# A recurrent cell over 256 steps: GpSimd also sums quarter 3, a new order of work, and TensorE's loop head at slot 0

## The reference, cut to what matters

```
encoded   = tanh(xt @ We + st @ Ue + be)                     # 24 values
new_state = tanh(xt @ Wx[c] + st @ Ws[c] + bk[c])            # 8 candidates of 32
mem       = [[encoded, err]] + mem[:-1]                      # the last 20 entries
agent_in  = relu(relu(mem @ enc_w1 + b1) @ enc_w2 + b2)      # 500 -> 64 -> 16
h1, c1    = lstm(agent_in, h1, c1);  h2, c2 = lstm(h1, h2, c2)
gate      = softmax(h2 @ gate_w + gate_b)
theta     = clamp01(2.5 * mean(|err| of the last 10 entries))
gate      = gate * theta + previous gate * (1 - theta)
st        = sum over c of gate[c] * new_state[c]
pred      = clamp01(st[31]);  err = pred - yt
```

## Time and profile before

| | us |
|---|---|
| median of 3 runs | 5925.37 (5924.08 to 5929.31) |
| the profiled execution | 5930.65 |
| its span | 5928.8 |
| TensorE busy / VectorE / ScalarE / GpSimd | 5535.1 / 4689.8 / 3831.1 / 1639.7 |
| mean granted TensorE clock | 0.979 of full speed |

### The profile page before, as it was taken

How to read it: one execution, slowest core, us unless ns; L and a number is a source line. 1 busy time by engine, 2 the same in 40 slices (tenths; PEclk the granted TensorE clock), 3 DMA queues, 4 the chain that set the end, 5 groups by cost and what they waited for, 6 DMA issues and landing times.

```text
span 5928.8 us, 184458 instructions
## 1 busy us (share of the span) xinstructions
PE 5535.1 (93%) x67584; PEld 3438.4 (58%) x67584; DVE 4689.8 (79%) x12854; ACT 3831.1 (65%) x9217; POOL 1639.7 (28%) x3588
## 2 busy tenths in 40 slices
PE   4999999999999999999999999999999999999998
PEld 2555555555555555555555555555555555555555
DVE  5878887887887887788788788788878878878887
ACT  2666666666666666666666666666666666666665
POOL 1222222222222222222222222222222222222222
PEclk9999999999999999999999999999999999999999
DMA  2111111111111111111111111111111111111111
GB/s 45 30 26 30 27 30 27 30 28 28 27 29 27 30 30 27 30 27 30 27 30 27 30 27 30 27 30 27 30 27 30 27 30 27 30 27 30 27 30 37
DMA packets 313074, 172.28 MB, mean 29 GB/s; under 512 B 171368, under 2 KB 278132, under 8 KB 312452
## 3 DMA queue, kind: packets, MB, share of 16 engines
q1 hardware_dynamic: 308724, 162.02, 10.4%
q10 hardware_dynamic: 3728, 0.15, 0.0%
HBM read 73.73 MB, written 2.10 MB: 13 GB/s over the span
## 4 chain that ended last, share of the span: by engine, by line
PE 71%; ACT 13%; DVE 9%; issue 6%; ACTq 1%; DMA 0%; POOL 0%; POOLq 0%; DVEq 0%
PE chain L442 16%; PE a_ps L404 10%; PE a_ps L393 8%; PE cand_ps L373 7%; PE cand_ps L364 7%; PE chain L429 6%; ACT a_sb L568 6%; ACT gates L593 4%; PE chain L338 4%; PE a_ps L415 4%; PE chain L459 4%; DVE cell_in L769 4%; DVE added L755 3%; PE cand_ps L359 3%; ACT tanh_c L599 2%
## 5 line engine op out<-in xcount | busy, mean ns | idle before, releaser
L393 PE MATMUL a_ps<-hist,w_hist 125*64 125x512 f16 x12288 | 1745.0, 389 | 80.9 <-DMA w_hist<-enc_table 80.9
L846 DVE TENSOR_REDUCE state<-mixed 128x64 f32<-128x512 f32 x2048 | 1353.3, 682 | 36.4 <-issue 2.4
L586 ACT ACTIVATE cand<-cand_ps 128x512 f32<-128x512 f32 x2048 | 1154.2, 590 | 184.6 <-PE cand_ps L373 184.6
L442 PE MATMUL chain<-cell_in,cell_w 128*64 128x128 f32 x16384 | 1092.9, 276 | 0.7 <-ACT cell_in L576 0.5
L442 PEld LDWEIGHTS chain<-cell_in,cell_w 128*64 128x64 f32 x16384 | 887.9, 136 | 288.8 <-ACT cell_in L576 181.4
L593 ACT ACTIVATE gates<-chain 128x512 f32<-128x512 f32 x1024 | 611.4, 597 | 619.7 <-PE chain L442 619.7
L959 POOL TENSOR_TENSOR err_ring<-pred_now,ys 128x8 f32 x512 | 122.0, 238 | 3129.6 <-DVE pred_now L853 3129.6
L393 PEld LDWEIGHTS a_ps<-hist,w_hist 125*64 125x64 f16 x12288 | 671.4, 112 | 526.1 <-issue 117.1
L755 DVE SCALAR_TENSOR_TENSOR added<-gates 128x256 f32<-128x256 f32 x1024 | 435.5, 425 | 445.2 <-ACT gates L593 445.2
L599 ACT ACTIVATE tanh_c<-gates 128x128 f32<-128x128 f32 x1024 | 316.9, 310 | 689.7 <-DVE gates L761 689.7
L769 DVE SCALAR_TENSOR_TENSOR cell_in<-gates,tanh_c 64x128 f32<-64x128 f32 x2048 | 585.7, 286 | 164.5 <-ACT tanh_c L599 150.9
(11 more groups left out here) (82 smaller groups left out, 6708.4 us busy)
## 6 DMA issues: line engine op xcount, KB each, us to landing
x_sb<-in_x_l SPq DMA_DIRECT2D x260, 256.0 KB, 2.8
hist<-entry_parts SPq DMA_DIRECT2D x2048, 25.0 KB
w_hist<-enc_table SPq DMA_DIRECT2D x258, 128.0 KB, 2.3
y_rows<-in_y_l SPq DMA_DIRECT2D x260, 8.0 KB
ys<-in_y SPq DMA_DIRECT2D x1, 2048.0 KB
preds_out<-preds SPq DMA_DIRECT2D x1, 2048.0 KB, 7.6
cell_w<-in_lstm_whh ACTq DMA_DIRECT2D x16, 3.0 KB
cell_w<-in_lstm_whh ACTq DMA_DIRECT2D x16, 1.0 KB
```

The source lines that it names most:

```text
L393: nc.tensor.matmul(a_ps[g][ENC * half:ENC * half + ENC, :], w_hist[0:HROWS, w_slot(u), kk, wp, :], hist[0:HROWS, xp, k, at:at + 512], star ...
L442: last = nc.tensor.matmul(chain[g][rows, P * r:P * r + P], cell_w[c][:, hf, r, :], cell_in[c][:, g, hf, :], start=False, stop=True, skip_g ...
L586: ins = nc.scalar.activation(cand[:, g, q // 2, :, q % 2, :, :].rearrange("p h s c -> p h (s c)"), cand_ps[q][:, :].rearrange("p (h k) -> ...
L846: V.tensor_reduce(state[:, g, hf, 2 * pair:2 * pair + 2, :], mixed[:, pair, hf, :, :, :], AX, ALU.add)\
```

## The change

- GpSimd gets `sum_of_quarter`: it adds the 8 candidates of quarter 3, both halves at once, by three additions (8 to 4, 4 to 2, 2 to 1), each waiting for the one before. `mix_sum` for pair 1 keeps quarter 2 alone. A semaphore `q_last` counts the new sums; `state_transpose`, `prediction` and the next `mix(1)` wait for it.
- The four phases of TensorE, ScalarE, VectorE and GpSimd are written in a new order, and some calls move from one item role to another (a call for `cur` that becomes one for `old` is made a phase later in the program).
- `CAND_ORDER` becomes (0, 2, 1, 3).
- TensorE's loop is given `head_slot` 0: its first instruction is to be loaded at slot 0 of an instruction fetch block.

```diff
+TENSOR_HEAD = 0
-CAND_ORDER = (2, 1, 3, 0)
+CAND_ORDER = (0, 2, 1, 3)
...
+        fours = sb("fours", [P, HF, S, 4])
+        twos = sb("twos", [P, HF, S, 2])
...
-            with nc.Fori(0, LOOPS, engines=[eng.engine], hint_back_edge=True) as turn:
+            with nc.Fori(0, LOOPS, engines=[eng.engine], hint_back_edge=True, head_slot=head_slot) as turn:
...
             def state_transpose(item, hf):
                 g, n, u = item
                 pe.wait_ge(q_sum[hf], SUMS * n)
+                pe.wait_ge(q_last, n)
```

TensorE's phase as it becomes (the old one is in the kernel above):

```diff
+                if old:
+                    cell_gates(old, 1)
+                if cur:
+                    state_transpose(cur, 0)
+                    state_transpose(cur, 1)
                 if new:
                     history_waits(new, old, extra)
                     history(new, 0)
+                if old:
+                    logit_bias(old)
+                if cur:
+                    encoded_s(cur)
+                if new:
+                    history(new, 1)
+                if old:
+                    gate_logits(old)
+                if cur:
+                    encoder1_now(cur)
+                    candidates_s(cur)
                     encoder2(cur)
                     bias_of_cell(cur, 0)
                 if new:
+                    history(new, 2)
                 if cur:
                     cell_gates(cur, 0)
+                if new:
+                    history(new, 3)
+                    encoded_x(new, old, extra)
+                if cur:
                     bias_of_cell(cur, 1)
                 if new:
+                    candidates_x(new, cur, extra)
+            run_phases(pe, phase, turn_start, {pe.engine: TENSOR_HEAD})
```

ScalarE's, and what is new on VectorE and GpSimd:

```diff
+                if old:
+                    candidates(old, 2)
+                    candidates(old, 1)
+                    cell_tanhs(old, 0)
+                    candidates(old, 3)
+                    value_tanh(old, 0)
+                    cell_tanhs(old, 1)
+                if cur:
+                    state_take(cur)
+                if old:
+                    value_tanh(old, 1)
+                if cur:
+                    at_least_zero(cur)
+                    encoded(cur)
+                if old:
+                    next_hidden(old)
+                if cur:
+                    entry_high(cur)
+                if old:
+                    exponentials(old)
+                if cur:
+                    encoder1(cur)
+                    candidates(cur, 0)
                     agent_input(cur)
...
+                if old:
+                    mix_sum(old, 0, 0)
+                if cur:
+                    cell_terms(cur, 0)
+                    cell_value(cur, 0)
+                if old:
+                    mix_sum(old, 0, 1)
                 if cur:
                     new_hidden(cur, 0)
                 if old:
+                    mix_sum(old, 1, 0)
                     mix_sum(old, 1, 1)
...
                 if cur:
                     peaks(cur)
                     below_peak(cur)
+                if new:
+                    error_sum(new)
+                    thetas(new)
+                if cur:
                     totals(cur)
...
+            def sum_of_quarter(item):
+                g, n, u = item
+                pool.wait_ge(q_mul[1], n + GROUPS if MIX_ORDER[1] == 1 else n)
+                G.tensor_tensor(fours[:, :, :, :], mixed[:, 1, :, 1, :, 0:4], mixed[:, 1, :, 1, :, 4:8], ALU.add)\
+                    .then_inc(q_fours, 1)
+                pool.wait_ge(q_fours, n)
+                G.tensor_tensor(twos[:, :, :, :], fours[:, :, :, 0:2], fours[:, :, :, 2:4], ALU.add)\
+                    .then_inc(q_twos, 1)
+                pool.wait_ge(q_twos, n)
+                G.tensor_tensor(state[:, g, :, 3, :], twos[:, :, :, 0], twos[:, :, :, 1], ALU.add)\
+                    .then_inc(q_last, 1)
...
                 if old:
-                    mix_quarter(old)
                     new_error(old, extra)
                     keep_prediction(old, extra)
-                if cur:
-                    kept_share(cur)
-                    kept_gate(cur)
                 if new:
                     entry_low(new)
                 if cur:
                     gate_in_sbuf(cur)
+                    mix_quarter(cur)
+                if new:
+                    kept_share(new)
+                    kept_gate(new)
+                if cur:
+                    sum_of_quarter(cur)
```

More of the change, by code:

```diff
@@ L140, in recurrent_kernel @@
                                     "inps", "in", "candps"))
+        q_fours, q_twos, q_last = (sem(f"q_{n}") for n in ("fours", "twos", "last"))
         q_keptfrom, q_mulpool = (sem(f"q_{n}") for n in ("keptfrom", "mulpool"))
@@ L160, in w_slot, with run_phases @@
             return u % PER_TILE
-        def run_phases(eng, phase, turn_start=None):
+        def run_phases(eng, phase, turn_start=None, head_slot=None):
             items = [None] * DEPTH
@@ L472, in phase @@
                 new, cur, old = items
+                if old:
+                    cell_gates(old, 1)
                 if cur:
-                    encoded_s(cur)
+                    state_transpose(cur, 0)
+                    state_transpose(cur, 1)
+                if new:
+                    history_waits(new, old, extra)
+                    history(new, 0)
                 if old:
@@ L482, in phase @@
                     encoder1_now(cur)
-                if new:
-                    history_waits(new, old, extra)
-                    history(new, 0)
-                if cur:
+                    candidates_s(cur)
                     encoder2(cur)
@@ L489, in phase @@
                 if new:
-                    history(new, 1)
+                    history(new, 2)
                 if cur:
                     cell_gates(cur, 0)
-                    candidates_x(cur, old, extra)
-                    candidates_s(cur)
+                if new:
+                    history(new, 3)
+                    encoded_x(new, old, extra)
+                if cur:
                     bias_of_cell(cur, 1)
                 if new:
[L497 to L505, removed]
+                    candidates_x(new, cur, extra)
+            run_phases(pe, phase, turn_start, {pe.engine: TENSOR_HEAD})
         @block.scalar
@@ L621, in phase @@
                 if cur:
[L622 to L628, removed]
-                if cur:
[L630 to L642, removed]
+                    entry_high(cur)
+                if old:
+                    exponentials(old)
+                if cur:
+                    encoder1(cur)
                     candidates(cur, 0)
+                    agent_input(cur)
             run_phases(act, phase)
@@ L845, in mix_sum @@
                     dve.wait_ge(q_mulpool, n + GROUPS)
-                V.tensor_reduce(state[:, g, hf, 2 * pair:2 * pair + 2, :], mixed[:, pair, hf, :, :, :], AX, ALU.add)\
-                    .then_inc(q_sum[hf], 1)
+                    V.tensor_reduce(state[:, g, hf, 0:2, :], mixed[:, 0, hf, :, :, :], AX, ALU.add)\
+                        .then_inc(q_sum[hf], 1)
+                else:
+                    V.tensor_reduce(state[:, g, hf, 2, :], mixed[:, 1, hf, 0, :, :], AX, ALU.add)\
+                        .then_inc(q_sum[hf], 1)
             def prediction(item):
@@ L864, in phase @@
                 if old:
-                    mix_sum(old, 0, 1)
+                    mix_sum(old, 1, 0)
                     mix_sum(old, 1, 1)
                 if cur:
-                    error_sum(cur)
                     cell_terms(cur, 1)
@@ L877, in phase @@
                 if cur:
-                    thetas(cur)
                     peaks(cur)
                     below_peak(cur)
+                if new:
+                    error_sum(new)
+                    thetas(new)
+                if cur:
                     totals(cur)
@@ L887, in phase @@
                     mix(cur, 0)
-                    mix_sum(cur, 1, 0)
-                if new:
-                    cell_terms(new, 0)
-                    cell_value(new, 0)
-                if cur:
-                    mix_sum(cur, 0, 0)
             run_phases(dve, phase, turn_start)
```

6 lines of the change are left out of this document (3 added, 3 removed).

## The result

The changed kernel takes 5894.02 us at the median of its runs (5892.56 to 5894.66), against 5927.12 for the kernel before, run again beside it (5924.08 to 5929.31): ratio 0.9944, 95% interval 0.9927 to 0.9961. So it is faster, by 33 us or 0.6%. The kernel before read 5925.9 to 5927.6 in the median beside every later group of runs, so times of different groups can be compared to about 2 us.

What follows compares the result with a forecast made beforehand. The prediction took the latency of a 10.93 us ring of dependent steps as the bound, plus stalls at loop back edges. 5930.65 - 220 + 138 = 5849, or 5843 as median; own range 5756 to 5889, 8-in-10 range 5735 to 5925.

Steps and rivals of the forecast that it cites:

- Ring: Chain of dependent steps from one second-cell gate tanh to the next: 10.93 us a phase, bound by latency.
- Part 1: TensorE's loop head at slot 0 starts its fetch well ahead of the branch: 220 us gained, bounds 0 to 226.
- Part 2: Quarter-3 sums moved from VectorE to GpSimd: VectorE's saving lies off the ring, GpSimd has slack, so 0.
- Rival B: GpSimd's sums hold up VectorE's cell terms: tie at 0.16 us a phase, slower beyond, 6201 at 0.7; chance 0.06.
- GpSimd pays: Where GpSimd's sums overlap VectorE's cell terms, GpSimd is the one slowed, and it has slack: cost 0.
- Part 3, +0.31 a phase: Agent input on ScalarE starts later, behind a candidate tanh waiting for TensorE's candidate product: +0.31 us, bounds +0.14 to +0.40.
- L415 is not what is late: TensorE's agent product ends at 3021.36, so its reader could start at 3021.43, before the candidate tanh frees ScalarE.
- Part 3, -0.04: The second cell's TensorE block starts straight from its wait: 1.14 us to its reader instead of 1.18.
- the stall only partly gone: Case where the loop's back-edge fetch stall only partly disappears: about 5900 to 5960 us, chance 0.07.
- +0.36: Upper bound of the new order's net cost per phase, forecast +0.27 (+138 us), bounds +0.10 to +0.36 (+184 us).

Runs made afterwards that it cites:

- b_head0: Kernel before with its loop head at slot 0 and nothing else changed: 5709.87 us, ratio 0.9633.
- a_slot89: Changed kernel with its loop head at slot 89 instead of 0: 6097.23 us, in one run.
- a_lowfirst: Changed kernel with agent_input's two halves in the other order, rows 0 to 63 first: 5818.22 us, ratio 0.9818.
- a_agentfirst: Changed kernel with agent_input ahead of the quarter-0 candidate tanh in ScalarE's order: 5818.47 us, ratio 0.9820.
- b_q3: Kernel before with loop head at slot 0 and quarter 3 summed by GpSimd, in the old order of work: 5704.97 us, ratio 0.9627.
- b_head0_x: b_head0 with TensorE's encoded_x moved from in front of the second cell to behind it: 5716.49 us, ratio 0.9649.
- b_q3_x: b_q3 with TensorE's encoded_x moved from in front of the second cell to behind it: 5658.00 us, ratio 0.9550.
- b_lowfirst: Kernel before with loop head at slot 0 and agent_input's halves in the other order: 5709.7 us, beside 5709.87 without the swap.
- a_nobias: Changed kernel with agent_input's two relus without their bias operand (enc_b2 left out of the result): 5797.38 us, ratio 0.9781.

## Why the prediction was wrong, point by point

The sum was 51 us too low. One term was mis-sized, the new order at ScalarE and TensorE, +0.31 a phase where +0.495 was measured; another, the sums, was put at nothing by a wrong reading of VectorE's new order, where -0.106 was measured. The two errors have opposite signs and partly cancel, so the total is nearer than its parts: that is luck. The time lies 5 us above the forecast's own upper end, 5889.

- **Ring, not engine load.** Right. The back edges aside, every gain and loss above is a step of the ring that got longer or shorter; the untouched steps stayed within 0.002.
- **Part 1, the slot, -220.** Right: -217 (b_head0), as argued (a_slot89): eleven fetches a turn, one of them begun 5 us ahead of the branch, the 3.55 us gone, and no slow stretch behind. What remains is a branch of 0.35 instead of the 0.1 that I allowed.
- **Part 2, the sums, 0.** This step failed, at "behind nothing that the ring waits for". I placed the halved reductions only behind the first cell's new hidden state. In the new order `mix_sum(old, 0, 1)`, half 0 of pair 1, stands *between* cell_value and new_hidden, and it is a halved one. There VectorE is late, so 0.106 a phase, 53 us, were on the ring. The prices on GpSimd held but one: 0.73 and 0.40 against 0.67 and 0.43, and 0.54 for the last against 0.30. The sums end at 3013.42, 2.2 us before the transpose at 3015.66 (slack forecast 2.1).
- **Rival B, contention with the cell terms.** Not so in 480 of the 512 pairs of L759 and GpSimd's last addition: L759 stays at 0.42. In 31 GpSimd starts first, and L759 takes 0.57 in the median. So it was close: see the last section. The prediction's "GpSimd pays" was read from one pair, in which VectorE starts first.
- **Part 3, +0.31 a phase.** The mechanism was right: the agent input waits for a candidate tanh that waits for L378. The size was off, 0.495. Of the 0.185 missing, 0.12 is the spacing of the agent input behind the tanh, 0.62 where I took 0.50 from two full tanhs (a_lowfirst gives back 0.129), and 0.07 is L378, which lasts 1.15 and not 1.08; why it does was not traced. Its start, 0.07 before L409's modelled end, was as forecast: L409 ends at 3008.51, L378 starts at 3008.44. "L415 is not what is late" was right too, and yet TensorE's part alone is 0.229 (forecast 0.16), as a_agentfirst shows; in the changed kernel the wait for the tanh hides it.
- **Part 3, -0.04.** Right: 3.702 to 3.668, -0.034, in the kernel with VectorE's sums. The second cell now starts from its wait, with nothing of TensorE in front.
- **Sum.** -217 + 237 - 53 = -33 us, the measured difference. The forecast had -220 + 138 + 0. The order of work cost 99 us more than I had said, and the sums gave 53 that I had not seen.

I named a time near 5900 only for "the stall only partly gone", with a chance of 0.07, and the stall was gone. The upper end of part 3's term, +0.36, lies below the measured +0.461 (0.495 less 0.034): there I was too sure, since a spacing of two *like* instructions was carried over to two unlike ones.

## What to carry to other kernels

In a kernel bound by latency, list for each instruction that you shorten or move which instruction stands next on the same engine and whether the ring waits for that one; a shortening pays there, and only if no other engine is late at the same point, as b_q3, b_head0_x and b_q3_x show (5 us gained by the one edit, 7 lost by the other, 52 gained by both). Test the parts of a bundled change apart: here one gained 217 us, one 53, and the third lost 237, so the whole looked like a small gain. Take the distance between two instructions only from a pair with the same rows and operands, and look in the trace for such a pair before you forecast.

## What the runs showed of the hardware

- **ScalarE overlapped two activations only when both began at the same row.** Behind a full tanh of 0.60 an activation on rows 64 to 127 started 0.62 us later, one on rows 0 to 63 0.50 later (a_lowfirst), as another full tanh does. The kept traces hold more pairs in which the second does not seem to wait for data. With the same first row the second started 0.10 *before* the first one's end: a cell tanh and `state_take`, `encoded` and `next_hidden`'s rows 0 to 63, agent input's rows 0 to 63 and a full tanh. With another first row it started 0.01 to 0.03 *behind* the end: `value_tanh` and `at_least_zero` (rows 96 to 99), `at_least_zero` and `encoded`, `next_hidden`'s rows 64 to 127 and `entry_high`, agent input's rows 64 to 127 and a full tanh (a_lowfirst), and the two halves of agent input in either order (0.363 long, 0.375 apart; b_lowfirst 0.362 and 0.375). The function did not matter. Why is open.
- **A bias operand costs 0.09 us** in an activation of 64x128 from PSUM (a_nobias: 0.375 against 0.283 from one to the next, and 0.363 against 0.272 in length).
- **Who loses when GpSimd and VectorE meet: the one that starts second, by the overlap less 0.14 us.** The Trainium skill (GPSIMD Engine Reference, Key points) says that they contend when the VectorE instruction has two SBUF inputs; the traces agree, and that list does not say who loses. Undisturbed, VectorE's cell terms take 0.425 and GpSimd's last addition 0.291. In the changed kernel VectorE starts 0.035 ahead (median of 480 phases), the two overlap by 0.39, and GpSimd's addition takes 0.54; in a_lowfirst it starts 0.18 ahead, they overlap by 0.25, and GpSimd takes 0.40; in a_nobias 0.22 ahead, 0.21 of overlap, and 0.36. In b_q3 GpSimd starts 0.06 ahead in 460 phases, the overlap is 0.23, and VectorE takes 0.515 while GpSimd keeps its 0.29. Each time the loss is the overlap less 0.14. The changed kernel's own trace has both outcomes, 480 phases the one way and 31 the other. No run was made for this alone, and other sizes were not tried. So rival B hung on less than a tenth of a microsecond of timing.
- **The slot of the loop head decides over 3.2 us a turn**, and with it over a stretch at half clock: a branch of 0.35 us and 564 fetches in all with the head at slot 0, 3.55 and 613 with it at slot 89.
